# A graph network's second edge stage: where a slot's second addition into the accumulator stands in VectorE's program

## The chip, the cores and the metric

The kernel runs on 1 core of a Trainium2 chip. The metric is the device time of one execution in microseconds (us); before the change three executions took 1823.59, 1826.35 and 1827.79 us (median 1826.35). The profiled execution took 1825.39 us, with a span of 1823.7 us in the trace.

## The reference

Two layers run one after the other on 3125 nodes of 256 numbers, each a graph stage over 50000 edges (sorted by destination) followed by a feed-forward stage. The change is in the edge part of the second graph stage:

```
mod_k  = K[src] + 0.2 * rel_w[edge_relations]
scores = (Q[dst] * mod_k).sum(per head) / sqrt(64)          # 4 heads of 64
seg_max = segment_max(scores, dst)
ex     = exp(scores - seg_max[dst]);  denom = segment_sum(ex, dst)
agg    = segment_sum(ex / denom[dst] * V[src], dst)
```

## The kernel before, in words

The edges are worked on in 416 steps of 128 edges, each step belonging to one window of 128 destination nodes. A lot is 32 steps (13 lots); a slot handles two steps, so that a lot has 16 slots, `q` = 0 to 15. Within one slot of lot `m` the two kinds of work are far apart in the steps: the scores are made for lot `m + 1`, steps 2q and 2q + 1, while the sums are taken for the steps `first` = 32m + 2q - 12 and `first + 1`.

The engines work at the same time, each through its own program in order, and hold to one another by semaphores:

- GpSimd (POOL) gathers the key and value rows of step t + 52 (line 1348) as soon as TensorE's sum of step t has been taken (`summed`). In every 16th step (t % 16 == 7) it also does the addition into the accumulator (line 1361), after waiting for all additions before it (`added`).
- TensorE (PE) makes the relation and query rows of the next pair (`look`, lines 1625 and 1632), then two sums (`add_up`, line 1672), each 128 x 260 numbers into one of NB = 3 PSUM banks. The sum of step t may start when step t - 3 has been added. Around a lot's change it also turns scores, tips, contexts and probabilities.
- VectorE (DVE) does per slot: `score_add` (keys plus relation, line 1389), `score_reduce` (line 1404, in 13 of 16 slots, the other three pairs are ScalarE's), `score_multiply` (keys times query, line 1396, waits for its `score_add`), and then the two additions `add(first)` and `add(first + 1)` (line 1486). Slots 1 to 4 hold the maxima of a lot besides, and slot 6 the rescaling of the accumulator.
- ScalarE (ACT) makes the exponentials (line 1565), the messages (line 1556), the three pairs' reductions and the copy of the sum that POOL adds (line 1583).
- SyncE loads the one-hot matrices and labels.

An addition waits for its sum (`summed`) and for the addition before it (`added`, since both may go to the same window).
Of the kernel before, what the change touches and what calls it, by code (L numbers as in the profile page):

```python
# [37 lines left out]
STEPS = -(-(TILES + WIN - 1) // (2 * BATCH)) * 2 * BATCH  # L38
# [22 lines left out]
class Chain:  # L61
# [23 lines left out]
    def wait(self):  # L85

        self.eng.wait_ge(self.sem, self.value())
# [1050 lines left out]
def edges_second(nc, k, ctx, acc):  # L1138
# [9 lines left out]
    FIRST_SUM = 12  # L1148
# [20 lines left out]
    def rows_at(t, count):  # L1169

        r = (t + SHIFT) % SLOTS2
        assert r + count <= OWN or OWN <= r and r + count <= SLOTS2
        return own[:, r:r + count, :] if r < OWN else spare[:, r - OWN:r - OWN + count, :]

    def pair_at(t):

        pair = t // QP
        return pair % ROWS_SEMS, 16 * QP * (pair // ROWS_SEMS + 1)
# [200 lines left out]
    def _(v):  # L1379
# [3 lines left out]
        def score_add(m, q):  # L1383
            t = m * LONG + q * QP
            keys = rows_at(t, QP)[:, :, 0:D].rearrange("p s (h f) -> p s h f", h=H)
            at, count = pair_at(t)
            v.wait_ge(related, m * PAIRS2 + (q + 1))
            v.wait_ge(rows_in[at], count)
            c.inc(v.tensor_tensor(keys, keys, ps_r[q % 2].unsqueeze(2).to_broadcast([P, QP, H, F]), ALU.add))  # L1389
            with_relation[m * PAIRS2 + q] = c.count  # L1390

        def score_multiply(m, q):
            v.wait_ge(k.dve_steps, with_relation[m * PAIRS2 + q])
            v.wait_ge(looked, m * PAIRS2 + (q + 1))
            keys = rows_at(m * LONG + q * QP, QP)[:, :, 0:D]
            v.tensor_tensor(keys, keys, ps_q[q % 2][:, :, :], ALU.mult).then_inc(look_used, 1)  # L1396

        def score_reduce(m, q):
            if q in ACT_PAIRS:
                return  # L1400
            at = slice(q * QP, (q + 1) * QP)
            v.wait_ge(look_used, m * PAIRS2 + (q + 1))
            keys = rows_at(m * LONG + q * QP, QP)[:, :, 0:D]
            v.tensor_reduce(sc2[:, at, :], keys.rearrange("p s (h f) -> p s h f", h=H), AX_X, ALU.add
                            ).then_inc(scored, 1)

        def scans(m, ini_f, ini_b):
            b = m % 2
            c.inc(v.tensor_tensor_scan(fwd[:, :], cut[b][:, 0:P], ps_t[:, 0:P], ini_f, ALU.add, ALU.max))
            c.inc(v.tensor_tensor_scan(bwd[:, ::-1], cut[b][:, P:0:-1], ps_t[:, P - 1::-1], ini_b, ALU.add, ALU.max))  # L1410
            return c.count

        def ends_of_steps(m, made):
            v.wait_ge(k.dve_steps, made)
            v.tensor_scalar(tip[:, 0, :], k.mask4[:, :], fwd[:, P - 1:P], None, ALU.mult)
            v.tensor_scalar(tip[:, 1, :], k.mask4[:, :], bwd[:, 0:1], None, ALU.mult).then_inc(tips, 1)

        def across_steps(m):
            lo = m * LONG
            v.wait_ge(by_head, 2 * m + 1)  # L1420
            c.inc(v.tensor_tensor_scan(run[:, lo + 1:lo + LONG + 1], k.joined[0:H, 1, lo:lo + LONG],
                                       ps_tip[:, 0:LONG], run[:, lo:lo + 1], ALU.add, ALU.max))
            c.inc(v.tensor_tensor_scan(back[:, LONG - 1::-1], k.joined[0:H, 2, lo:lo + LONG][:, ::-1],
                                       ps_tip[:, 2 * LONG - 1:LONG - 1:-1], NEG, ALU.add, ALU.max))
            return c.count

        def context_rows(m, made):
            lo = m * LONG
            v.wait_ge(k.dve_steps, made)
            c.inc(v.tensor_tensor(ctxt[:, 0, :], run[:, lo:lo + LONG], k.joined[0:H, 0, lo:lo + LONG], ALU.add))  # L1430
            c.inc(v.tensor_tensor(ctxt[:, 1, :], back[:, 1:LONG + 1], k.joined[0:H, 0, lo + 1:lo + LONG + 1], ALU.add))
            contexts_made[m] = c.count

        def newest_maximum(m):
            v.wait_ge(k.dve_steps, contexts_made[m])
            c.inc(v.tensor_tensor(new_max[:, :], back[:, 0:1], ctxt[:, 0, 0:1], ALU.max))
            return c.count

        def fall_of_maximum(m, made):
            v.wait_ge(k.dve_steps, made)  # L1440
            v.tensor_scalar(fall[:, :], ctxt[:, 0, 0:1], new_max[:, 0:1], -80.0, ALU.subtract, ALU.max
                            ).then_inc(by_vector, 1)

        def factors(m):
            v.wait_ge(factor_ready, m)
            v.scalar_tensor_tensor(out=diag[:, :], in0=k.ident[0:H, 0:H], scalar=factor[:, 0:1],
                                   in1=k.ident[0:H, 0:H], op0=ALU.mult, op1=ALU.subtract).then_inc(by_vector, 1)

        def contexts(m):
            v.wait_ge(by_head, 2 * m + 2)  # L1450
            c.inc(v.tensor_tensor(ini2[:, :, :], ps_ctx.rearrange("p (j s) -> p j s", j=2),
                                  k.mask4[:, :].unsqueeze(1).to_broadcast([P, 2, LONG]), ALU.mult))
            return c.count

        def reduce_contexts(made):
            v.wait_ge(k.dve_steps, made)
            c.inc(v.tensor_reduce(ini[:, :], ini2[:, :, :], AX_X, ALU.add))
            return c.count

        def maxima(made):  # L1460
            v.wait_ge(k.dve_steps, made)
            c.inc(v.tensor_tensor(fwd[:, :], fwd[:, :], bwd[:, :], ALU.max))
            return c.count

        def differences(made):
            v.wait_ge(k.dve_steps, made)
            v.tensor_tensor(diff[:, :], ps_t[:, 0:P], fwd[:, :], ALU.subtract).then_inc(diff_ready, 1)
# [11 lines left out]
        def add(t, w):  # L1479
            if t < 0 or t in pool_no:  # L1480
                return
            v.wait_ge(summed, t + 1)
            if t % LONG == LONG - 2 and t + 2 < STEPS:
                c.inc(v.tensor_copy(fac[:, :], bank[t % NB][:, FAC:FAC + H]))
            wait(v, added, t)
            v.tensor_tensor(acc[:, w[t % 8], :], acc[:, w[t % 8], :], psm[t % NB], ALU.add).then_inc(added, 1)  # L1486
# [9 lines left out]
        w = None  # L1496
        for m in range(LOTS2):
            more = m + 1 < LOTS2
            for q in range(PAIRS2):
                first = m * LONG + 2 * q - FIRST_SUM  # L1500
                if more:
                    score_add(m + 1, q)
                if q == 1:
                    v.wait_ge(transposed, 2 * m + 1)
                    v.wait_ge(cut_in, 16 * max(m + 1, 2))
                    made = scans(m, NEG, NEG)
                elif q == 2:
                    made = across_steps(m)
                elif q == 3:
                    made = contexts(m)  # L1510
                elif q == 4 and m:
                    factors(m)
                if q == 0:
                    score_reduce(m, PAIRS2 - 1)
                elif more:
                    score_reduce(m + 1, q - 1)
                if q == 1:
                    ends_of_steps(m, made)
                elif q == 2:
                    context_rows(m, made)  # L1520
                elif q == 3:
                    made = reduce_contexts(made)
                if more:
                    score_multiply(m + 1, q)
                if first >= 0 and first % 8 == 0:
                    w = load_windows(first, 8)
                if q == 2 and m:
                    made = newest_maximum(m)
                elif q == 3:
                    v.wait_ge(k.dve_steps, made)  # L1530
                    made = scans(m, ini[:, 0:1], ini[:, 1:2])
                if first == m * LONG and m:
                    v.wait_ge(k.dve_steps, c.count)
                    rescale(m, w[0])
                add(first, w)
                if q == 2 and m:
                    fall_of_maximum(m, made)
                elif q == 3:
                    made = maxima(made)
                add(first + 1, w)  # L1540
                if q == 3:
                    differences(made)
        for t in range(STEPS - FIRST_SUM, STEPS):
            if t % 8 == 0:
                w = load_windows(t, 8)
            add(t, w)
# [1563 lines left out]
```

## Time and profile before

| | |
|---|---|
| median of 3 executions | 1826.35 us |
| profiled execution | 1825.39 us, span 1823.7 us |
| busy in the span: PE, DVE, ACT, POOL | 72%, 77%, 54%, 61% |
| second edge stage, about 1034 to 1595 us of the span | DVE 9 tenths in its slices |
| DMA, mean over the span | 201 GB/s; 261 to 273 in the slices of this stage up to 1550 us |

The shares are averages over stages with different limits: DVE's 77% over the whole span says little, the slices of the stage say that DVE is busy nine tenths there, and the question is what the last tenth is. The profile's chain of work that ended last follows only the final feed-forward stage, behind the one that is changed, so the stage is read from its waits and its timeline.

### The profile page before, as it was taken

The numbers are of one execution on the slowest core, as the hardware profiler recorded it, in microseconds if no ns is written. First come the engines' busy times: TensorE is split into PE (matmuls) and PEld (weight loads), VectorE is DVE, ScalarE is ACT, GpSimd is POOL, SyncE is SP. The second block draws the span as 40 slices with busy tenths as digits, with TensorE's granted clock in tenths as the row PEclk, the third lists the DMA queues.
The fourth block names the chain that finished last, engine by engine and source line by source line (L and its number), as shares of the span: only waits on it lengthen the run. The fifth ranks groups of instructions, "written<-read, shape, count | busy, mean of one in ns | idle before, by whom it ended". The sixth has DMA issues, their size and how long they took to land. (4 is left out here: it accounts for less than half of the span.)

```text
span 1823.7 us, 29715 instructions
## 1 busy us (share of the span) xinstructions
PE 1314.4 (72%) x7043; PEld 902.9 (50%) x7043; DVE 1397.3 (77%) x3568; ACT 992.8 (54%) x3802; POOL 1106.1 (61%) x1127
## 2 busy tenths in 40 slices
PE   6346666766666568999886888888888788777086
PEld 5223433434334466777553555555555555455075
DVE  6558888888889862564876899999999999785344
ACT  3345556555555352333252588888888888345043
POOL 3577777777777200574425776767767667474556
PEclk9668877778888758999997699999999999986588
DMA  5566777777776209532247888888888888446392
GB/s 152 154 185 209 216 207 220 214 208 210 221 214 192 82 0 300 198 125 84 93 167 241 267 262 270 273 265 272 271 262 270 268 268 261 137 134 137 146 332 69
DMA packets 176346, 367.26 MB, mean 201 GB/s; under 512 B 28663, under 2 KB 65608, under 8 KB 176052
## 3 DMA queue, kind: packets, MB, share of 16 engines
q0 software_dynamic: 58192, 175.85, 31.7%
q1 hardware_dynamic: 113989, 186.10, 31.0%
q10 hardware_dynamic: 4000, 3.41, 0.6%
q8 instruction: 67, 1.10, 0.2%
q14 instruction: 98, 0.80, 0.2%
HBM read 275.24 MB, written 94.15 MB: 203 GB/s over the span
## 5 line engine op out<-in xcount | busy, mean ns | idle before, releaser
L833 POOL DMA_INDIRECT e_rows<-h_rows,src_col x416 | 399.6, 961 | 138.7 <-issue 119.3
L1111 PE MATMUL e_sum<-e_rows,e_of_dst 128*128 128x264 f32 x832 | 308.6, 499 | 112.8 <-DVE e_rows L932 85.7
L1348 POOL DMA_INDIRECT e_rows<-kv_rows,src_col x320 | 302.7, 946 | 118.8 <-issue 70.3
L1556 ACT ACTIVATE e_rows<-e_rows 128x64 f32<-128x64 f32 x1152 | 281.1, 335 | 0.3
L1111 PEld LDWEIGHTS e_sum<-e_rows,e_of_dst 128*128 128x128 f32 x832 | 165.7, 233 | 177.3 <-DVE e_rows L932 91.4
L1632 PE MATMUL e_query<-q,e_to_dst 128*128 x1248 | 205.0, 295 | 64.3 <-DVE e_rows L1396 45.9
L1486 DVE TENSOR_TENSOR acc<-acc,e_sum 128x260 f32 x393 | 165.5, 421 | 44.7 <-DVE acc L1486 31.6
L1672 PE MATMUL e_sum<-e_rows,e_of_dst 128*128 128x260 f32 x640 | 183.4, 409 | 2.3 <-POOL e_rows L1280 1.7
L1632 PEld LDWEIGHTS e_query<-q,e_to_dst 128*128 128x128 bf16 x1248 | 120.9, 100 | 122.5 <-issue 83.4
L1036 ACT ACTIVATE e_rows<-e_rows 128x32 f32<-128x32 f32 x832 | 181.0, 305 | 0.1
L1348 POOL DMA_INDIRECT x<-kv_rows,src_col x96 | 90.9, 947 | 74.8 <-POOLq L2195 38.1
L2036 POOL TENSOR_SCALAR labels<-labels,typ_no 128x1024 bf16<-128x1024 bf16 x26 | 78.4, 3018 | 80.6 <-DMA labels<-step_typ 80.5
L1672 PEld LDWEIGHTS e_sum<-e_rows,e_of_dst 128*128 128x128 f32 x640 | 108.8, 191 | 24.6 <-DVE acc L1486 10.5
L1389 DVE TENSOR_TENSOR e_rows<-e_rows,e_relation 128x512 f32<-128x512 f32 x160 | 108.9, 681 | 8.5 <-DMA e_rows<-kv_rows,src_col 8.3
L1396 DVE TENSOR_TENSOR e_rows<-e_rows,e_query 128x512 f32<-128x512 f32 x160 | 108.5, 678 | 1.0
L942 DVE TENSOR_TENSOR acc<-acc,e_sum 128x264 f32 x208 | 87.2, 419 | 26.5 <-PE e_sum L1111 22.6
L1625 PEld LDWEIGHTS e_relation<-rel,e_to_typ 64*128 64x128 bf16 x1248 | 50.5, 97 | 95.4 <-issue 54.7
L932 DVE TENSOR_TENSOR e_rows<-e_rows,e_probabilities 128x512 f32<-128x512 f32 x148 | 96.1, 677 | 0.8
L1625 PE MATMUL e_relation<-rel,e_to_typ 64*128 64x64 bf16 x1248 | 75.0, 196 | 28.7 <-issue 8.8
L2053 PE MATMUL ps_h<-xt,w 128*128 128x320 f32 x320 | 91.2, 444 | 5.6 <-ACT hid L2073 3.1
L1556 ACT ACTIVATE x<-x 128x64 f32<-128x64 f32 x380 | 93.2, 334 | 0.1
L2062 PE MATMUL ps_y<-w,hid 128*128 128x256 f32 x400 | 87.6, 380 | 3.2 <-ACT hid L2073 3.2
(433 smaller groups left out, 2790.9 us busy)
## 6 DMA issues: line engine op xcount, KB each, us to landing
step_of<-e_of_dst SPq DMA_DIRECT2D x104, 256.0 KB
e_of_dst<-step_of SPq DMA_DIRECT2D x104, 256.0 KB, 4.2
sorted_rows<-zeros SPq DMA_DIRECT2D x1, 14560.0 KB
comb<-sorted_rows SPq DMA_DIRECT2D x56, 260.0 KB
e_rel<-step_rel SPq DMA_DIRECT2D x26, 512.0 KB, 4.3
step_to<-e_to_dst SPq DMA_DIRECT2D x26, 512.0 KB
e_to_dst<-step_to SPq DMA_DIRECT2D x52, 256.0 KB
e_rows<-h_rows,src_col POOLq DMA_INDIRECT x416
```

The costliest lines, as they stand in the source:

```text
L833: pool.indirect_dma_start(out=g[t // BATCH % R][:, t % BATCH, :], out_offset=None, in_=k.h_rows[:, :], in_offset=bass.IndirectOffsetOnAxis ...
L932: ins = v.tensor_tensor(vals, vals, pr.unsqueeze(3).to_broadcast([P, GROUP // 2, H, F]), ALU.mult)
L1036: ins = act.activation(x, x, ACT.Copy, scale=row[:, D + h:D + h + 1])
L1111: pe.matmul(psm[t % NB], of_dst[q][:, s % GROUP, :], g[m % R][:, s, :], start=True, stop=True).then_inc(summed, 1)
L1348: pool.indirect_dma_start(out=rows_at(t, 1)[:, 0, :], out_offset=None, in_=k.kv_rows[:, :], in_offset=bass.IndirectOffsetOnAxis(ap=k.src_c ...
L1389: c.inc(v.tensor_tensor(keys, keys, ps_r[q % 2].unsqueeze(2).to_broadcast([P, QP, H, F]), ALU.add))
L1396: v.tensor_tensor(keys, keys, ps_q[q % 2][:, :, :], ALU.mult).then_inc(look_used, 1)
L1486: v.tensor_tensor(acc[:, w[t % 8], :], acc[:, w[t % 8], :], psm[t % NB], ALU.add).then_inc(added, 1)
L1556: ins = act.activation(x, x, ACT.Copy, scale=row[:, plo + h:plo + h + 1])
L1625: mm = pe.matmul(ps_r[q % 2][:, t, :], to_typ[h // 2 % 2][typ, s * P:(s + 1) * P], k.by_typ[typ, j, :], start=(j == 0), stop=(j == 2))
L1632: mm = pe.matmul(ps_q[q % 2][:, t, :], to_dst[h % 2][:, s * P:(s + 1) * P], k.by_dst[:, w[t], j, :], start=(j == 0), stop=(j == 2))
L1672: pe.matmul(psm[t % NB], of_dst[q % GROUPS][:, s % GROUP, :], rows_at(t, 1)[:, 0, plo:R1], start=True, stop=True).then_inc(summed, 1)
```

## The change

Within a slot DVE no longer issues `add(first)` and `add(first + 1)` behind each other. The second addition of a slot is issued in the next slot, behind that slot's `score_add`; after the last lot's last slot one more is issued for what is left over.

```
@@ -1500,6 +1500,7 @@
                 first = m * LONG + 2 * q - FIRST_SUM
                 if more:
                     score_add(m + 1, q)
+                add(first - 1, w)
                 if q == 1:
@@ -1537,9 +1538,9 @@
                     fall_of_maximum(m, made)
                 elif q == 3:
                     made = maxima(made)
-                add(first + 1, w)
                 if q == 3:
                     differences(made)
+        add(STEPS - FIRST_SUM - 1, w)
         for t in range(STEPS - FIRST_SUM, STEPS):
```

DVE's program in an ordinary slot (slot 7 of a lot and the start of slot 8; `e_rows` are gathered rows, `e_sum` a PSUM bank, `acc` the accumulator), before:

```order
L1389 TENSOR_TENSOR e_rows<-e_rows,e_relation 128x2x256 [waits e1_rows_in4,e1_related]
L1404 TENSOR_REDUCE e_scores<-e_rows 128x8 [waits e1_look_used]
L1396 TENSOR_TENSOR e_rows<-e_rows,e_query 128x2x256 [waits e1_looked,dve_steps]
L1486 ISA [waits e1_added,e1_summed]
L1486 TENSOR_TENSOR acc<-acc,e_sum 128x260
L1486 ISA [waits e1_added,e1_summed]
L1486 TENSOR_TENSOR acc<-acc,e_sum 128x260
L1389 TENSOR_TENSOR x<-x,e_relation 128x2x256 [waits e1_rows_in5,e1_related]
```

The same place after:

```order
L1389 TENSOR_TENSOR e_rows<-e_rows,e_relation 128x2x256 [waits e1_rows_in4,e1_related]
L1486 ISA [waits e1_added,e1_summed]
L1486 TENSOR_TENSOR acc<-acc,e_sum 128x260
L1404 TENSOR_REDUCE e_scores<-e_rows 128x8 [waits e1_look_used]
L1396 TENSOR_TENSOR e_rows<-e_rows,e_query 128x2x256 [waits e1_looked,dve_steps]
L1486 ISA [waits e1_added,e1_summed]
L1486 TENSOR_TENSOR acc<-acc,e_sum 128x260
L1389 TENSOR_TENSOR x<-x,e_relation 128x2x256 [waits e1_rows_in5,e1_related]
```

Between any two additions now stands a pass over the keys. In slot 3 of a lot (`e_fwd` the maxima, `e_diff` what ScalarE's exponentials wait for), before:

```order
L1486 TENSOR_TENSOR acc<-acc,e_sum 128x260
L1462 TENSOR_TENSOR e_fwd<-e_fwd,e_bwd 128x128 [waits dve_steps]
L1486 ISA [waits e1_added,e1_summed]
L1486 TENSOR_TENSOR acc<-acc,e_sum 128x260
L1467 TENSOR_TENSOR e_diff<-e_turned,e_fwd 128x128 [waits dve_steps]
```

The same place after:

```order
L1486 TENSOR_TENSOR acc<-acc,e_sum 128x260
L1462 TENSOR_TENSOR e_fwd<-e_fwd,e_bwd 128x128 [waits dve_steps]
L1467 TENSOR_TENSOR e_diff<-e_turned,e_fwd 128x128 [waits dve_steps]
L1389 TENSOR_TENSOR e_rows<-e_rows,e_relation 128x2x256 [waits e1_rows_in1,e1_related]
L1486 ISA [waits e1_added,e1_summed]
```

The differences now stand directly behind the maxima, on which they wait. No other engine's program is changed.

## Rows read from the trace of the kernel before

**Rows 1.** Busy us of each engine, granted clock, DMA share, GB/s, by stretch

```profile
core 0: us, PE busy (x) PEld busy (x) DVE busy (x) ACT busy (x) POOL busy (x), PEclk, DMA share, GB/s
1040.00:1560.00 520.00, 420.33 (x3000) 280.69 (x2999) 482.44 (x1079) 433.96 (x2093) 360.24 (x388) 0.98 0.82 265
1364.00:1383.00 19.00, 14.89 (x107) 9.91 (x106) 17.70 (x37) 17.96 (x89) 14.16 (x15) 1.00 0.89 293
```

**Rows 2.** Waits, 1040 to 1560 us: us in total, times, longest us

```profile
ACT e_prob L1565 <- DVE e_diff L1467: 43.7, 11, 4.3
PE e_query L1632 <- DVE e_rows L1396: 41.6, 71, 0.9
ACT e_taken L1583 <- PE e_sum L1672: 37.4, 23, 3.1
DVE acc L1486 <- DVE acc L1486: 29.3, 134, 0.6
...
PE e_sum L1672 <- DVE acc L1486: 2.1, 2, 1.4
```

**Rows 3.** DVE in order of time: start, us, line, operation [idle before <-releaser]

```profile
1317.77 0.68 DVE L1389 TENSOR_TENSOR e_rows<-e_rows,e_relation 128x512 f32<-128x512 f32 x1
...
1318.97 0.68 DVE L1396 TENSOR_TENSOR e_rows<-e_rows,e_query 128x512 f32<-128x512 f32 x1
1319.56 0.42 DVE L1486 TENSOR_TENSOR acc<-acc,e_sum 128x260 f32 x1
1320.19 0.43 DVE L1486 TENSOR_TENSOR acc<-acc,e_sum 128x260 f32 x1 [0.21 <-DVE acc L1486]
1320.53 0.68 DVE L1389 TENSOR_TENSOR e_rows<-e_rows,e_relation 128x512 f32<-128x512 f32 x1
1321.24 0.69 DVE L1396 TENSOR_TENSOR e_rows<-e_rows,e_query 128x512 f32<-128x512 f32 x1
```

**Rows 4.** The same view, in slot 3 of a lot

```profile
1298.18 0.28 DVE L1462 TENSOR_TENSOR e_fwd<-e_fwd,e_bwd 128x128 f32<-128x128 f32 x1
1298.47 0.43 DVE L1486 TENSOR_TENSOR acc<-acc,e_sum 128x260 f32 x1
1298.81 0.28 DVE L1467 TENSOR_TENSOR e_diff<-e_turned,e_fwd 128x128 f32<-128x128 f32 x1
```

**Rows 5.** POOL in order of time, the whole stage

```profile
1034.86 0.94 POOL L1348 DMA_INDIRECT x<-kv_rows,src_col  x1 [0.30 <-issue]
...
1064.70 0.73 POOL L1361 TENSOR_TENSOR acc<-acc,e_taken 128x260 f32 x1 [0.77 <-DVE acc L1486]
...
1292.09 0.74 POOL L1361 TENSOR_TENSOR acc<-acc,e_taken 128x260 f32 x1 [1.24 <-DVE acc L1486]
...
1315.43 0.75 POOL L1361 TENSOR_TENSOR acc<-acc,e_taken 128x260 f32 x1
1316.34 0.95 POOL L1348 DMA_INDIRECT e_rows<-kv_rows,src_col  x1 [0.16 <-issue]
...
1335.12 0.95 POOL L1348 DMA_INDIRECT x<-kv_rows,src_col  x1 [0.30 <-PE e_sum L1672]
1337.35 0.74 POOL L1361 TENSOR_TENSOR acc<-acc,e_taken 128x260 f32 x1 [1.28 <-DVE acc L1486]
...
1520.31 0.73 POOL L1361 TENSOR_TENSOR acc<-acc,e_taken 128x260 f32 x1 [1.34 <-DVE acc L1486]
...
1549.48 0.95 POOL L1348 DMA_INDIRECT e_rows<-kv_rows,src_col  x1 [0.30 <-issue]
```

**Rows 6.** PE in order of time, one slot without a wait

```profile
1316.77 0.34 PE L1625 MATMUL e_relation<-rel,e_to_typ 64*128 64x64 bf16 x6
...
1318.92 0.34 PE L1625 MATMUL e_relation<-rel,e_to_typ 64*128 64x64 bf16 x6
```

**Rows 7.** Gather of step 43 on POOL

```profile
1023.61 0.95 POOL L1348 DMA_INDIRECT e_rows<-kv_rows,src_col  x1 [0.30 <-issue]
```

**Rows 8.** `score_add` of steps 42 and 43 on DVE

```profile
1029.10 0.69 DVE L1389 TENSOR_TENSOR e_rows<-e_rows,e_relation 128x512 f32<-128x512 f32 x1 [1.17 <-DMA e_rows<-kv_rows,src_col]
```

More of the change, by code:

```diff
@@ L1502, in _ @@
                     score_add(m + 1, q)
+                add(first - 1, w)
                 if q == 1:
@@ L1539, in _ @@
                     made = maxima(made)
-                add(first + 1, w)
                 if q == 3:
                     differences(made)
+        add(STEPS - FIRST_SUM - 1, w)
         for t in range(STEPS - FIRST_SUM, STEPS):
```

## The prediction, made before the changed kernel ran

> **What bounds the kernel now.** The chain of work that ended last is all in the final feed-forward stage, so I read the changed stage from three other views. First the busy times by stretch: between 1040 and 1560 us VectorE (DVE) is busy 482 of 520 us, TensorE (PE) 420, ScalarE (ACT) 434, GpSimd (POOL) 360 by its records [rows 1]. Then the waits of that stretch [rows 2]. ACT idles 43.7 + 37.4 us for the differences and for sums, PE 41.6 us for DVE's product with the query. Nobody waits long for PE or ACT, and DVE's largest wait is for itself: 29.3 us in 134 places, before an addition, until the addition ahead of it is done. Last the order in time. In a steady slot DVE runs without any other gap, 2.76 us from one `score_add` to the next (1317.77 to 1320.53) [rows 3], where PE needs 2.15 us when nothing holds it (1316.77 to 1318.92) [rows 6]. So DVE sets the pace of the slots.
>
> POOL's 360 us mislead: its gathers show 0.95 us, but the next starts 1.25 us after the last, whatever else goes on. From the addition at 1315.43 it takes 0.91 us to the next gather, 18.78 us for 15 more (1316.34 to 1335.12) and 0.95 us until it could add again: 20.64 us for 16 steps. It added only at 1337.35, after 1.28 us of waiting for DVE [rows 5]. Two halves make a lot, so POOL can't go below 41.3 us a lot. The lots now take (1520.31 - 1064.70) / 10 = 45.56 us [rows 5]. POOL is the next bound, 9% away.
>
> **The change part by part.** No work is added or removed; 13 lots' second additions move. Four terms.
>
> *The pairs of additions.* From the first addition to the second 0.63 us pass (1319.56 to 1320.19), from the second to the next `score_add` 0.34 us (1320.53). The addition lasts 0.42 us and the idle behind it is 0.21 us [rows 3]. Where nothing depends on the addition before, the next instruction starts 0.34 us after it. After the change `score_add` stands there, at +0.34 us, and the moved addition comes 0.59 us later (as a product follows by 0.59 at 1318.97 to 1319.56), at +0.93. What it depends on is over at +0.63, so the wait is covered with 0.30 us to spare. Each such place saves 0.63 - 0.34 = 0.29 us, more than the idle of 0.21, because the overlap of neighbours comes back too. 134 places [rows 2] give 38.9 us; 12 of a lot's 16 slots are such.
>
> *Slots without a reduction.* In three slots of a lot `score_multiply` follows its `score_add` directly and waits for it: 0.71 us (1320.53 to 1321.24) in place of 0.59 [rows 3]. The moved addition now fills that gap: 0.12 x 3 x 11 = 4.0 us.
>
> *Slot 3.* The addition used to lie between the maxima and the differences. They stood 0.63 us apart (1298.18 to 1298.81) [rows 4]. Now the differences wait for the maxima directly. The lower end is the maxima's own 0.28 us, the upper end is 0.28 + 0.21 = 0.49 with the idle of an addition [rows 3, 4]. The slot loses the difference between that and the 0.34 that an addition costs less the 0.29 it saves: between 0.1 us gained and 0.2 lost, 11 times. I take nothing, and keep -1 to +2 us. ACT gets its differences 0.1 to 0.3 us earlier, which is of use to nobody who is late. In slot 2 a small instruction lies between the additions already and I count nothing. The rescaling in slot 6 loses no cover.
>
> *Who waits for the moved addition.* PE's sum three steps on needs the bank. The bank comes free 0.34 + 0.59 - 0.63 = 0.30 us later than before, measured from the first addition. PE waited for an addition twice in 520 us, 2.1 us [rows 2], since its sum goes by the product with the query long after; with 2.15 us of work in a new slot of 2.47 it stays under [rows 3, 6]. Queued behind the moved addition's wait on DVE are the reduction and the product, and its sum was taken a slot earlier. POOL's own addition (every 16th step) waits for the first one of a pair, which isn't moved, and the other queues (SP's too) are passed by nothing.
>
> DVE alone would then save 38.9 + 4.0 = 42.9 us.
>
> **What is late next.** I set the halves of a lot against each other. The half without the lot's change takes 21.92 us now (1315.43 to 1337.35) [rows 5]. In it DVE saves 7 x 0.29 + 0.12 = 2.15, to 19.8, and POOL needs 20.64: POOL binds. The other half takes 45.56 - 21.92 = 23.64 on the mean. There DVE saves 5 x 0.29 + 0.24 = 1.69, to 21.95, and DVE binds. If neither can carry its lead over, a lot takes 20.64 + 21.95 = 42.6 us and saves 3.0. If it carries fully, the lot takes the larger of 41.3 and 45.56 - 3.84 = 41.7 and saves 3.8. POOL is held from the first gather released by a sum to the last, 1034.86 to 1549.48, 514.6 us or 11.3 lots [rows 5]: 34 us saved in the one case, 43 in the other. Rows are gathered 52 steps ahead, but POOL's addition ties the two engines within a slot or so twice a lot, so I take the middle, 38 us. The profiled execution's 1825.4 less 38 is 1787.4; it ran 1 us below the median of the three, so I forecast 1788.
>
> **The rivals.**
>
> *Nothing is won (0.07, 1826 us).* The idle before the second addition would be the flush of the first and would follow it wherever it stands. Against it: behind the second addition an instruction that depends on nothing starts after 0.34 us, not 0.63 [rows 3]. The Trainium skill (VectorE: DVE Perf Modes, "The DRAIN you can't avoid") states just such a rule: a pipeline flush after every op, and a chain with a semaphore after each op as fast as one without, so that "the semaphore costs nothing extra here". By that rule 1826 it would be. The trace disagrees at this place, 0.63 against 0.34 us. Also in this case falls a lot paced by the chain over its change (tips, contexts, exponentials). Against that, ACT waits some 4 us per lot for the differences and has 434 us of work, PE 420 [rows 1, 2]: both floors lie below POOL's 11.3 x 41.3 = 467.
>
> *The gathers come too late (0.27, 1800 to 1814 us).* The stage would need its bytes in less time: 265 GB/s x 520 / 482 = 286 GB/s. A 19 us stretch ran at 293 with a DMA share of 0.89 [rows 1], so the rate is there but near its top. The time from issue to use is tighter. The gather of step 43 started at 1023.61 and its rows, which DVE was waiting for, were used at 1029.10: 5.5 us [rows 7, 8]. With POOL late, the first gather behind its addition starts 0.9 us after the addition, and its rows are used after 0.74 + 0.2 (addition and release), 0.34 and two slots of 2.47: 6.2. That leaves 5.3 us, against 5.5 needed. If rows take 1 us longer under the denser load, DVE waits up to 1.2 us twice a lot, up to 27 us, of which I leave half to two thirds: 38 shrinks to 11 to 25. For it: DVE waited for rows wherever POOL was the slower. Against: in the dense 19 us no row of DVE waits for DMA.
> The Trainium skill (DMA: Bandwidth & Descriptors, "Where 436 GB/s comes from") puts the limit of HBM for one core at some 358 GB/s; by it 286 would be no bound, and an estimate from its fit (2.0 us plus bytes over 436 GB/s, "Anatomy of one DMA") is 2.6 us for 262 KB, where the trace shows 5.5.
>
> *Slower (0.03, about 1867 us if everywhere).* The three banks: the second bank is given back 0.30 us later. If PE's sum three steps on were always waiting for it, every slot would last 0.30 us longer instead of less: 0.30 x 12 x 11.3 = 41 us. It decides when PE reaches its sums before the addition two slots back is done. For it only that banks are few; against it the 2 waits of 2.1 us [rows 2] and 0.6 us of PE's idle in a slot.
>
> *That it doesn't do what it says* I exclude by the order: one addition stands in front of each pass, and between two additions there is always a `score_add`.
>
> **How the numbers follow.** The forecast has 0.63, with a range of its own from 1779 (43 us, the 1 to 2 us of slot 3, and shorter waits for sums) to 1796 (34 us saved, less some friction). The late gathers have 0.27, nothing won 0.07, slower 0.03. The range 1778 to 1811 leaves out the last two and a part of the late gathers. What a measurement of this kernel can tell from no change is 0.2%, some 3.7 us. Faster by more: 0.63 + 0.27 and a little of the third case, 0.91; within: 0.05; slower: 0.04.
>
> **What would show it.** Right: DVE's waits for its own addition fall from 134 places to hardly any in the stage; a steady slot without POOL's hold is 2.47 us; POOL's waits for sums shrink, its gathers run at 1.25 us nearly throughout, and between its additions lie 20.6 and about 22 us; first waits of DVE for POOL's addition or for gathered rows appear. The stage from 1034 us ends some 38 us earlier and all before and behind it keeps its length. Wrong: a moved addition with an idle of 0.2 us before it (nothing won), `score_add` waiting for DMA by 1 us twice a lot (late gathers), PE waiting for additions in most slots (banks).

## The result, and the profile after

| | before | after |
|---|---|---|
| median | 1826.14 us (1823.59 to 1827.79, 4 runs) | 1794.33 us (1793.41 to 1796.69, 4 runs) |
| profiled execution, span | 1825.39 us, 1823.7 us | 1793.41 us, 1791.6 us |
| first to last gather released by a sum | 514.6 us | 484.65 us |
| half of a lot with the lot's change, mean of 10 | 23.63 us | 21.88 us |
| the other half, mean of 10 | 21.93 us | 20.81 us |

The ratio is 0.983 (95% interval 0.981 to 0.984): under 2% and clear of the spread, 31.8 us less where 38 were forecast, and inside the range. The changed stage gave 30.0 of them.

Waits in the kernel after, 1040 to 1520 us (engine, line, waited for: us in total, times, longest us), to be held against [rows 2]:

```profile
PE e_query L1633 <- DVE e_rows L1396: 39.9, 63, 1.3
ACT e_prob L1566 <- DVE e_diff L1467: 35.2, 11, 3.6
POOL e_rows L1348 <- PE e_sum L1673: 33.8, 87, 1.1
...
DVE e_rows L1389 <- DMA e_rows<-kv_rows,src_col: 9.9, 9, 1.6
...
DVE acc L1486 <- POOL acc L1361: 5.0, 12, 1.0
...
DVE x L1389 <- DMA x<-kv_rows,src_col: 2.6, 4, 0.9
...
PEld e_sum L1673 <- DVE acc L1486: 0.2, 1, 0.2
```

DVE's 134 waits for its own addition are gone. In their place stand 12.5 us in 13 places for gathered rows and 5.0 us in 12 places for POOL's addition. The busy times by stretch (answering to [rows 1]; the short ones are used further down):

```profile
core 0: us, PE busy (x) PEld busy (x) DVE busy (x) ACT busy (x) POOL busy (x), PEclk, DMA share, GB/s
1040.00:1520.00 480.00, 399.31 (x2969) 273.85 (x2968) 460.61 (x1062) 426.02 (x2053) 357.38 (x384) 0.99 0.87 285
1299.00:1302.00 3.00, 2.41 (x23) 1.63 (x20) 2.79 (x6) 3.00 (x22) 2.23 (x3) 1.00 0.95 337
1302.00:1305.50 3.50, 3.50 (x26) 2.57 (x25) 1.96 (x5) 3.50 (x16) 2.59 (x4) 1.00 0.94 332
```

The same bytes in less time: 285 GB/s at a DMA share of 0.87, where it was 265 at 0.82. DVE in order of time, slots 10 to 15 of a lot and slot 3 of the next (start, us, line, operation, idle before and releaser), answering to [rows 3]:

```profile
1299.21 0.42 DVE L1486 TENSOR_TENSOR acc<-acc,e_sum 128x260 f32 x1 [0.28 <-POOL acc L1361]
...
1302.01 0.68 DVE L1389 TENSOR_TENSOR e_rows<-e_rows,e_relation 128x512 f32<-128x512 f32 x1
1302.61 0.42 DVE L1486 TENSOR_TENSOR acc<-acc,e_sum 128x260 f32 x1
1302.94 0.68 DVE L1396 TENSOR_TENSOR e_rows<-e_rows,e_query 128x512 f32<-128x512 f32 x1
...
1305.55 0.69 DVE L1389 TENSOR_TENSOR e_rows<-e_rows,e_relation 128x512 f32<-128x512 f32 x1 [1.59 <-DMA e_rows<-kv_rows,src_col]
...
1308.02 0.68 DVE L1389 TENSOR_TENSOR e_rows<-e_rows,e_relation 128x512 f32<-128x512 f32 x1
1308.62 0.42 DVE L1486 TENSOR_TENSOR acc<-acc,e_sum 128x260 f32 x1
1308.95 0.68 DVE L1404 TENSOR_REDUCE e_scores<-e_rows 128x8 f32<-128x512 f32 x1
1309.55 0.68 DVE L1396 TENSOR_TENSOR e_rows<-e_rows,e_query 128x512 f32<-128x512 f32 x1
1310.14 0.42 DVE L1486 TENSOR_TENSOR acc<-acc,e_sum 128x260 f32 x1
1310.48 0.68 DVE L1389 TENSOR_TENSOR e_rows<-e_rows,e_relation 128x512 f32<-128x512 f32 x1
...
1325.08 0.28 DVE L1462 TENSOR_TENSOR e_fwd<-e_fwd,e_bwd 128x128 f32<-128x128 f32 x1
1325.39 0.29 DVE L1467 TENSOR_TENSOR e_diff<-e_turned,e_fwd 128x128 f32<-128x128 f32 x1
```

A steady slot takes 2.46 us (1308.02 to 1310.48, forecast 2.47). In the slot without a reduction the product follows its `score_add` after 0.93 us with the whole addition between them (before, 0.71 with nothing). In slot 3 the differences follow the maxima after 0.31 us, before after 0.63 [rows 4]. The one gap is at 1305.55: 1.59 us for rows. POOL, answering to [rows 5]:

```profile
1062.71 0.74 POOL L1361 TENSOR_TENSOR acc<-acc,e_taken 128x260 f32 x1
...
1298.25 0.75 POOL L1361 TENSOR_TENSOR acc<-acc,e_taken 128x260 f32 x1
1299.16 0.95 POOL L1348 DMA_INDIRECT e_rows<-kv_rows,src_col  x1 [0.16 <-PE e_sum L1673]
...
1319.15 0.74 POOL L1361 TENSOR_TENSOR acc<-acc,e_taken 128x260 f32 x1 [0.29 <-DVE acc L1486]
...
1341.14 0.76 POOL L1361 TENSOR_TENSOR acc<-acc,e_taken 128x260 f32 x1
...
1489.65 0.74 POOL L1361 TENSOR_TENSOR acc<-acc,e_taken 128x260 f32 x1
```

Ten lots take (1489.65 - 1062.71) / 10 = 42.69 us each, where they took 45.56. The late rows at 1305.55 belong to the gather that starts at 1299.16, right behind POOL's addition: 6.4 us from start to use, while the DMA moved 337 and 332 GB/s at shares of 0.95 and 0.94.

### The profile page after: what moved, and what is told of

It is laid out like the page before. It is cut to its first block and busy times, and to the rows that moved or that the text cites. A ratio compares the mean times of both kernels' runs of the same rounds, so it can differ in the third digit from the quotient of the medians.

```text
span 1791.6 us, 29715 instructions
## 1 busy us (share of the span) xinstructions
PE 1297.4 (72%) x7043; PEld 898.8 (50%) x7043; DVE 1385.0 (77%) x3568; ACT 992.2 (55%) x3802; POOL 1107.7 (62%) x1127
## 5 line engine op out<-in xcount | busy, mean ns | idle before, releaser
L1633 PE MATMUL e_query<-q,e_to_dst 128*128 x1248 | 197.3, 292 | 58.9 <-DVE e_rows L1396 45.7
L1633 PEld LDWEIGHTS e_query<-q,e_to_dst 128*128 128x128 bf16 x1248 | 117.0, 100 | 107.8 <-issue 72.0
```

Source lines behind the costliest of these rows:

```text
L1633: mm = pe.matmul(ps_q[q % 2][:, t, :], to_dst[h % 2][:, s * P:(s + 1) * P], k.by_dst[:, w[t], j, :], start=(j == 0), stop=(j == 2))
```

## The experiments

All were timed beside the kernel before on the same chips (medians 1826.25 to 1827.56 us). "Lot" below is the distance from one new maximum on DVE to the next; by it a lot took 45.25 us before and 42.42 after. Times 11.3 lots the difference is 32 us. "Late rows" are DVE's waits for gathered rows between 1040 and 1520 us.

**One half of a lot at a time.** With the moved addition in slots 2 to 8 alone, which hold the lot's change (a slot not in MOVED adds where it did before):

```
+        MOVED = (2, 3, 4, 5, 6, 7, 8)
...
+                if (q - 1) % PAIRS2 in MOVED:
+                    add(first - 1, w)
...
+                if q not in MOVED:
+                    add(first + 1, w)
```

> The change in slots 2 to 8 of each lot only (the half with the lot's change); in slots 10 to 15 and 0 both additions stand behind each other as before. Theory 1: the half with the lot's change is VectorE's, saves 5 x 0.29 + 0.24 = 1.7 us a lot, 19 us in all, 1807; the other half stays at 21.9 us with POOL waiting 1.3 us for VectorE. Theory 2 (the transfers' rate): also 1807, as the stage stays below the rate of the full change. If the lot's change were paced by the chain over the exponentials: 1815 or more.

Measured 1812.99 us, ratio 0.992 (0.990 to 0.993): 14.6 us, between the 19 us of DVE's own saving (1807) and the 1815 of a half paced by the exponentials. The halves take 22.71 and 21.51 us, 0.92 and 0.42 less than before. The same with `MOVED = (10, 11, 12, 13, 14, 15, 0)`, the other half:

> The change in slots 10 to 15 and 0 of each lot only. VectorE saves 7 x 0.29 + 0.12 = 2.15 us a lot there. Theory 1: POOL allows only 21.9 - 20.6 = 1.3 us of it, 14 us in all, 1812, unless VectorE's lead is carried into the next half; the sum of this one and the other half alone gives the whole change's 32 us. Theory 2 (rate of the transfers) or 3 (VectorE alone): 2.15 us a lot, 24 us, 1802, and the two parts together would be more than the whole.

Measured 1808.96 us, ratio 0.990 (0.988 to 0.992): 18.6 us. Here the halves take 23.33 and 20.81 us, 0.30 and 1.12 less. That lies between the two forecasts, 1812 and 1802. The two parts together give 33.2 us, the whole 31.8. So the parts add up within the spread, and of what one moved half saves, a third or less shows in the half that was left as it was.

**POOL's additions, which tie the two engines.** Taken away, so that DVE does all of them:

```
-    by_pool = [t for t in range(TAIL) if t % BATCH == 7]
+    by_pool = []
```

> The change, and besides POOL adds nothing: VectorE does every 16th step's addition too, ScalarE's copy of that sum goes. Theory 1 (POOL's queue of gathers and additions, 20.6 us for 16 steps, paces the half of a lot without the lot's change): POOL is freed of 2 x 0.62 us a lot and falls to 40.0 us, VectorE has 2 x 0.34 us more and alone would need some 42.4 us a lot against 42.7 measured with the change; VectorE's waits for POOL and for gathered rows nearly vanish, POOL waits for sums in both halves, time 1788 to 1794. Theory 2 (the transfers' rate paces the stage): nothing of the transfers is changed, VectorE still waits for rows, 1794 or a little more. Theory 3 (VectorE paces both halves already): plus 0.68 us a lot, 1802.

Measured 1799.09 us, ratio 0.984 (0.982 to 0.985). DVE never waits for POOL now and POOL has slack, yet the time is no better. The 1788 to 1794 of a half paced by POOL are out; 1799 lies between the 1794 or a little more of the transfers and the 1802 of DVE alone. The waits of this kernel:

```profile
POOL e_rows L1348 <- PE e_sum L1673: 53.5, 101, 2.3
...
DVE e_rows L1389 <- DMA e_rows<-kv_rows,src_col: 8.2, 10, 1.2
DVE x L1389 <- DMA x<-kv_rows,src_col: 3.2, 3, 1.6
```

Rows are late by 11.4 us although no addition of POOL delays a gather. With `t % BATCH == 11`, away from the sum that POOL waits for:

> The change, and POOL adds the steps with t % 16 == 11 instead of 7. Theory 1b (a lot is POOL's own 2 x 20.6 us plus 1.4 us in which its gathers wait for the sums of steps 28 and 30, late by the chain over differences and exponentials): one of POOL's two additions now falls into that wait, right ahead of the gather that waits for sum 28, and costs nothing: 0.6 us a lot less, 7 us in all, 1787 to 1790. Theory 2 (the transfers' bursts pace the stage through late rows): POOL's place doesn't matter, 1794. If POOL's addition of step 27 delays the differences' chain: over 1797.

Measured 1798.50 us, ratio 0.984 (0.982 to 0.986): a miss for the 1787 to 1790 of the first theory, and in the range of the third. The waits:

```profile
DVE acc L1486 <- POOL acc L1361: 12.6, 11, 1.8
POOL acc L1361 <- DVE acc L1486: 11.9, 11, 1.4
```

POOL's addition of step 27 now waits for DVE's addition of step 26, in slot 3, and the gather behind it is held back. DVE's late rows fell to 3.8 us in 6 places here, and the time is no better: what the rows gave, the tie took. With one addition a lot (`t % LONG == 23`):

> The change, and POOL adds one step in 32 (t % 32 == 23) instead of two. The loop of a lot that I read (POOL's addition 7, released VectorE, the differences, the chain to sum 28, POOL's 11 gathers to the next addition 7: 42.0 us plus late rows) is cut at addition 7: POOL has 0.62 us less and VectorE 0.34 us more. If that loop sets the time: a lot falls to about 42.3 us (VectorE's own 41.3 plus 1 us of late rows), 1789 to 1792. If late rows are all that matters: 1794 or more, as without any of POOL's additions (1799).

Measured 1796.44 us, ratio 0.983 (0.980 to 0.985), lot 42.63, late rows 14.9 us in 15 places. Half of the tie is gone and the time isn't better, as the second forecast had it. The late rows grew by 2.4 us and DVE has 12 more additions; that these took what the tie gave is argued, not shown.

**Another order.** The product with the query between the two additions, in the kernel before (in slot 3 the scans are moved behind the first addition as well, which the lines below leave out):

```
-                if more:
-                    score_multiply(m + 1, q)
...
                 add(first, w)
+                if more:
+                    score_multiply(m + 1, q)
...
                 add(first + 1, w)
```

> The kernel before, but inside a slot the order is: first addition, product with the query, second addition. Nothing crosses the slot's end. The idle between the additions is covered by the product (0.59 us). If the gain is the cover of the wait and nothing else, the 0.21 us idles vanish as with the change and the time is near the changed kernel's: 1794, up to 1803 if the first addition, now 0.6 us earlier in the slot, waits for PE's sum in the slots without a reduction. If the idle is a flush that follows every addition (rival: nothing is won by an order), 1826; if the later return of the PSUM bank or the later second sum matters, the time differs from the changed kernel's by more than 10 us.

Measured 1849.90 us, ratio 1.012 (1.010 to 1.015). The forecast had a case for a time more than 10 us off, but none in which the kernel gets slower than before. DVE in order of time:

```profile
1370.18 0.68 DVE L1396 TENSOR_TENSOR e_rows<-e_rows,e_query 128x512 f32<-128x512 f32 x1
1370.78 0.42 DVE L1486 TENSOR_TENSOR acc<-acc,e_sum 128x260 f32 x1
1371.11 0.68 DVE L1389 TENSOR_TENSOR e_rows<-e_rows,e_relation 128x512 f32<-128x512 f32 x1
1372.61 0.43 DVE L1486 TENSOR_TENSOR acc<-acc,e_sum 128x260 f32 x1 [0.82 <-PE e_sum L1672]
1372.95 0.68 DVE L1396 TENSOR_TENSOR e_rows<-e_rows,e_query 128x512 f32<-128x512 f32 x1
...
1379.36 0.68 DVE L1389 TENSOR_TENSOR e_rows<-e_rows,e_relation 128x512 f32<-128x512 f32 x1
1380.90 0.42 DVE L1486 TENSOR_TENSOR acc<-acc,e_sum 128x260 f32 x1 [0.86 <-PE e_sum L1672]
...
1382.17 0.68 DVE L1389 TENSOR_TENSOR e_rows<-e_rows,e_relation 128x512 f32<-128x512 f32 x1
```

and PE:

```profile
1371.00 0.94 PE L1632 MATMUL e_query<-q,e_to_dst 128*128 x6 [0.59 <-DVE e_rows L1396]
1371.78 1.11 PE L1672 MATMUL e_sum<-e_rows,e_of_dst 128*128 128x260 f32 x4
```

The waits for its own addition are gone here too, but a loop has closed: product (1370.18), PE's query rows (1371.00), PE's sums behind them (1371.78), the first addition (1372.61), and only then the next product (1372.95): 2.77 us a slot. DVE's additions wait 42.6 us in 110 places for sums, in the kernel after 0.5 us in 2.

A slot with a reduction took 2.76 us before as well, so this loop takes back there what the cover gives and no more. The time above the kernel before comes from elsewhere. Slot 12, which has no reduction, takes 2.81 us (1379.36 to 1382.17), where the kernel before takes 2.29 (from 1320.53 [rows 3] to the next `score_add`):

```profile
1322.82 0.68 DVE L1389 TENSOR_TENSOR e_rows<-e_rows,e_relation 128x512 f32<-128x512 f32 x1
```

In the mean of ten lots slot 12 takes 0.5 us more, slot 9 (no reduction either) 0.8 and slots 5 and 10 some 0.4 each. Slot 6 takes 0.4 less, and a lot 2.0 more, or 22 us in all. Slots 5, 6 and 10 were not traced further. So what counts isn't only that something stands between the additions, but what: here the product, on which PE waits, stands behind an addition that waits for PE.

**Fewer bytes.** In the kernel after, SyncE loads 16 of 1024 columns of the relation labels once the first chunks are in; the relation labels of the later steps are left out.

```
-            sp.dma_start(to_typ[h // 2 % 2][:, :], ...
+            cols = CHUNK * P if h < 4 else 16
+            sp.dma_start(to_typ[h // 2 % 2][:, 0:cols], ...
```

> The change, and the relation labels (256 KB every 16 steps, issued by SyncE together with 256 KB of destination labels) are loaded in full only twice, afterwards 16 of 1024 columns: this leaves out most of the labels, some 4% of the stage's bytes and the burst in front of the late gather. Theory 2 (rows are late because the gather stands behind SyncE's burst, and this eats the lead that VectorE has in the other half): VectorE's waits for rows, 12.5 us now, fall below 5 us, the lead is carried into the lot's change, POOL's waits for sums 28 and 30 shrink: 1784 to 1788. Theory 1b alone (the lot is set by POOL and the chain over the differences, and the waits for rows lie in POOL's shadow): 1794.

Measured 1790.74 us, ratio 0.981 (0.978 to 0.983), lot 42.08, late rows 5.7 us at 274 GB/s: not quite the under 5 us and 1784 to 1788 of the second theory, and not the 1794 of the other. The same edit in the kernel before:

> The kernel before, with the relation labels' loads made small as in the run before this. VectorE waits for no rows there, so whatever the theory the time stays at the kernel before's, 1826 +- 2. A gain of more than 4 us would mean that the transfers slow the engines in another way than by late rows.

Measured 1827.76 us, ratio 1.001 (0.999 to 1.002): the bytes cost nothing there. In the kernel after, with nothing left out, the relation labels loaded with the odd chunk, so that no two loads of 256 KB go out together:

> The change, and the relation labels are loaded one half earlier, with the odd chunk of destination labels, so that SyncE's 512 KB every 16 steps become 256 KB every 8 steps; nothing is left out. Theory 2 (burst): VectorE's waits for rows in slot 13 of a lot shrink from 1.0 to 1.6 us to under 0.5 and the time falls to 1785 to 1790. If it is the mean rate and not the burst: waits move to other slots and the time stays at 1794. Theory 1b alone: 1794.

Measured 1794.04 us (four executions, 1791.45 to 1804.19), ratio 0.983 (0.979 to 0.987), late rows 14.5 us in 17 places. Spread out, the late rows only turn up elsewhere. That points to the rate in the mean and not to one burst. The kernel after itself, again, for the spread:

> The changed kernel once more, on the chip of the next two, to compare them with it: 0.9826 of the kernel before, lots of 42.7 us with 0.5 to 1.6 us of waiting for rows in each.

Measured 1797.47 us, ratio 0.983 (0.981 to 0.986), late rows 11.7 us. The interval of the kernel with fewer bytes overlaps this one, so its gain of some 4 to 7 us is likely, not certain.

**More rows in flight.** Without POOL's additions ScalarE's copies fall away, and with two more buffers shared there is room for 54 steps of rows in place of 52:

```
-    OWN, SPARE = 40, 12
+    OWN, SPARE = 42, 12
...
-    diff = sb("diff", [P, P])
-    prob = sb("prob", [P, P])
+    diff = bwd
+    prob = fwd
...
-    by_pool = [t for t in range(TAIL) if t % BATCH == 7]
+    by_pool = []
```

> The change without POOL's additions (as measured before: 1799 us, lots of 43.1 us, VectorE waits 11.4 us for rows), and besides 54 instead of 52 rows in flight, so that each gather may be issued two steps, some 2.6 us, earlier; the space comes from ScalarE's copies that are not needed then and from two tiles that share storage. Late rows cost time (theory 2): the waits for rows vanish, the lot falls from 43.1 by the 1.0 us that it waited for them to 42.1 to 42.3, 1787 to 1791. Late rows lie in another wait's shadow: 1797 to 1800 as before.

Measured 1783.24 us, ratio 0.975 (0.973 to 0.977), the fastest of all, 4 us below the forecast for late rows that cost time, and 16 us below the run with 52 rows and no addition on POOL. Its busy times and waits:

```profile
1040.00:1520.00 480.00, 408.52 (x3004) 277.20 (x3003) 475.48 (x1109) 428.68 (x2079) 344.54 (x365) 0.99 0.86 287
```

```profile
DVE e_rows L1388 <- DMA e_rows<-kv_rows,src_col: 2.1, 3, 1.2
...
DVE acc L1485 <- DVE acc L1485: 0.6, 3, 0.2
```

At the same density (0.86, 287 GB/s) the rows are late by 2.1 us, not 11.4, and DVE is busy 475.5 of 480 us (463.5 with 52). The gathers themselves land no sooner, with a median of 4.6 and 4.8 us from issue (for the two kinds of buffers) where it was 4.5 and 4.8: what helps is that they start earlier. The 9.3 us of late rows account for a part of the 16 us; DVE's waits for sums, 3.7 us with 52 rows, are 0.9 here, and the rest was not traced. The new maxima in the two kernels (durations in ns, first and last start in us), 52 rows:

```profile
L1436 DVE TENSOR_TENSOR e_new_max<-e_back,e_ctxt x12: 140/141/147, 1067.0 to 1536.6; 4x1 f32<-4x1 f32 x12
```

and 54:

```profile
L1435 DVE TENSOR_TENSOR e_new_max<-e_back,e_ctxt x12: 140/141/148, 1065.8 to 1520.9; 4x1 f32<-4x1 f32 x12
```

Eleven lots, 42.69 and 41.37 us each. The same kernel with 54 rows and the additions in the old order, right behind each other:

> 54 rows in flight and no additions by POOL as in the run e10 (1783 us, lots of 41.4 us), but with the old order: a slot's two additions behind each other. If the moved addition's covered wait is what the rest builds on, VectorE alone sets the pace again and has 2 x 0.63 us a lot more than before: lots of about 46.5 us, 1838 to 1843 us, no waits for rows. If most of e10's gain came from the rows in flight whatever the order: below 1815.

Measured 1842.79 us, ratio 1.008 (1.006 to 1.011):

```profile
DVE acc L1485 <- DVE acc L1485: 30.6, 140, 0.6
```

So the room for rows and the rest of that edit are worth nothing alone. Without the moved additions they cost 16 us, which is the first forecast (1838 to 1843): POOL's additions are DVE's now, at 0.63 us each in the old order. On top of them the moved additions bring some 60 us.

## Why the prediction was right, and where 6 us went

*What bounds, and the four terms.* DVE did set the pace. Each pair gave what was forecast: 0.29 us (from 0.63 to 0.34), a steady slot of 2.46 for 2.47. The slots without a reduction came out as reckoned (0.60 + 0.33, nothing idle). Slot 3 lies near the lower end, 0.31 us between 0.28 and 0.49, and counted at nothing is right. By the forecast's own terms the slot could win only 0.63 - 0.34 - 0.28 = 0.01 us, not 0.1; nothing hangs on it. PE waited 0.2 us for an addition: the rival of the banks is out.

*Nothing won.* The Trainium skill (VectorE: DVE Perf Modes, "The DRAIN you can't avoid") says that the next operation does not start until the pipe is empty; by that alone the gap would follow the addition wherever it stands. The same section adds that a next operation that is not held starts earlier, which the forecast left out. In the kernel after, what follows an addition without waiting starts 0.33 to 0.34 us after it, in every ordinary slot shown. Here the wait did cost, 0.29 us a place.

*The halves.* The forecast set POOL's 20.64 against DVE's 19.8 in the one half, and DVE's 21.95 in the other. Measured are 20.81 and 21.88. This is the case "neither can carry its lead over", 3.0 us a lot; 2.87 came. The step that failed is the next one, "so I take the middle, 38 us": it let half of the lead be carried, and put no late rows into the likeliest case. By it 38, by the no-carry end 34, measured 31.8. The forecast's own signs, 20.6 and about 22 us between POOL's additions, already summed to the no-carry 42.6.

*Why nothing was carried.* The runs with one half moved show that a lead can pass: 0.3 to 0.4 us of it a lot appear in the half that was left as it was. In the whole change late rows stood in its way, at least in part. A lot in which no wait for rows is recorded (from POOL's addition at 1338.79 us of the run with fewer bytes) takes 42.05 us: 0.96 to DVE's addition, 25.32 to the differences, 1.74 to the gather that follows them and 14.03 to POOL's next addition. The one of the kernel after from 1298.25 to 1341.14 takes 42.89, with 1.59 us for rows. That kernel too has a lot nearly as short as 42.05: 42.09 us from 1383.58 to 1425.67, with 0.7 us for rows. At 42.05 in all lots (45.56 - 42.05) x 11.3 = 40 us would have been saved, and (42.69 - 42.05) x 11.3 = 7 us is what the mean lot loses against such a lot. Both are worked out, not run, and that late rows took all of the 7 is not shown. That late rows limit the new order the runs do show: cutting the tie to POOL alone gave nothing (1796.4 and 1799.1), fewer bytes halved the late rows and gave a few us (likely, not certain), and two more steps of rows in flight nearly removed them and gave 16 in the kernel without POOL's additions. They are not the only limit, since with few late rows (3.8 us) but longer waits between DVE and POOL the time was 1798.5.

The other piece of the no-carry result is POOL's in the lot's change, which the forecast gave to DVE alone. POOL's gathers in that half, in the kernel after:

```profile
1327.13 0.94 POOL L1348 DMA_INDIRECT e_rows<-kv_rows,src_col  x1 [1.15 <-PE e_sum L1673]
1328.38 0.95 POOL L1348 DMA_INDIRECT e_rows<-kv_rows,src_col  x1 [0.30 <-issue]
1330.19 0.94 POOL L1348 DMA_INDIRECT e_rows<-kv_rows,src_col  x1 [0.86 <-PE e_sum L1673]
```

Twice it waits for a sum, which waits for the exponentials behind DVE's differences. From there 14.0 us of gathers, hardly held, lead to its addition at 1341.14. So the half runs through DVE first and POOL after. That neither could shorten it alone is read from this order, not run.

*The gathers come too late.* This rival, an either-or at 0.27, was half true. The place it named is there (5.3 us left, 5.5 needed, 6.4 taken), and a wait is 1.0 us in the mean (12.5 / 13), close to its 1.2. But it happens once a lot, not twice, and the run without POOL's additions has as many. POOL's addition isn't needed for it; what the runs leave is rows that are only 52 steps ahead at 285 GB/s. It should have been a term of the forecast, not a case beside it. Its price was also mis-worked: half to two thirds of 27 us taken from 38 leave 20 to 25 us saved, and the 11 us at which its range ends (1814) take all 27.

*Open.* 54 rows with both of POOL's additions kept had no room and was not run. From the old order to the new with 54 rows a lot shrinks by 5.15 us (46.52 to 41.37, by the same eleven lots); the pairs explain 4.3 of it (13.7 waits a lot at 0.29, and 0.36 for the slots without a reduction), and the rest was not traced.

## What to carry to other kernels

An idle of 0.2 us between two dependent operations is worth more than it shows, since the overlap with the neighbour comes back as well: read it from start to start. But look at what goes between: an operation on which the additions' producer waits, put behind an addition that itself waits for that producer, closes a loop (1849.9 us here). And when a stage runs faster with the same bytes, count the depth of the prefetch in time, not in steps: 52 steps ahead were enough at 45.6 us a lot and no longer at 42.7, and two more steps (16 us) were worth more than anything else that was tried on top of the new order.

## What the runs showed that was not expected

- A gather on which DVE waited took 5.5 us from start to use before the change [rows 7, 8], with 308 GB/s moved at a share of 0.88 between 1023.6 and 1029.1 us, and 6.4 us after it, at 332 to 337 GB/s and 0.94 to 0.95. These are two single gathers.
- The relation labels' bytes cost nothing before (ratio 1.001) and likely some us after: a transfer is free only at a given pace.
- DVE's addition for POOL is nearly free for the whole: 23 more additions on DVE (some 0.34 us each, 7.8 us) moved the time by 2 to 5 us, which the intervals don't tell from none.
